# DLRM tower on one core: layer matmuls placed among those of the Gram, ids in three parts, weights loaded behind the tables

## What is computed

```python
e = jnp.stack([tbl_0[ids[:, 0]], ..., tbl_26[ids[:, 26]]], axis=1)
dot = jnp.einsum('bnd,bmd->bnm', e, e)
z = dot.reshape(2048, 27 * 27)[:, idx]      # idx: the pairs i < j
h = jnp.concatenate([z, dense_ctx], axis=1)
h = jnp.maximum(h @ W_top1 + b_top1, 0.0)
h = jnp.maximum(h @ W_top2 + b_top2, 0.0)
y = h @ W_top3
```

## Time and profile before

| | us |
|---|---|
| median of 3 runs | 417.63 (416.83 to 418.69) |
| the profiled execution | 419.41 |
| its span, first to last instruction | 417.6 |
| busy: PE / DVE / POOL / ACT | 348.4 / 276.0 / 262.4 / 159.7 |

### The profile page before, as it was taken

One profiled execution on the slowest core, in us unless ns is written; L12 is line 12 of the kernel. 1 busy time (PEld: TensorE's weight loads), 2 busy tenths in 40 slices (PEclk: granted clock), 3 DMA queues, 4 the chain that ended last, 5 costly groups with the idle time before them and its releaser, 6 DMA issues.

```text
span 417.6 us, 15062 instructions
## 1 busy us (share of the span) xinstructions
PE 348.4 (83%) x6092; PEld 312.5 (75%) x6092; DVE 276.0 (66%) x741; ACT 159.7 (38%) x221; POOL 262.4 (63%) x277
## 2 busy tenths in 40 slices
PE   0277686799979998899989998999899998899766
PEld 0266576689859897789778986898688976897565
DVE  0647954796765965896579677787479748952410
ACT  0827961223432334422442343334422334234422
POOL 5777417777477737677777767767777677770000
PEclk9978675999998999999999999999999999999889
DMA  4799995362425233245524352419333562210000
GB/s 82 176 254 249 222 82 85 65 99 64 99 54 110 52 74 84 58 90 71 113 58 102 58 111 52 109 32 85 98 75 82 66 108 56 54 53 14 3 3 0
DMA packets 29611, 35.51 MB, mean 85 GB/s; under 512 B 12729, under 2 KB 23617, under 8 KB 29586
## 3 DMA queue, kind: packets, MB, share of 16 engines
q1 hardware_dynamic: 20882, 17.32, 26.6%
q0 software_dynamic: 8704, 17.84, 15.7%
HBM read 35.13 MB, written 0.01 MB: 84 GB/s over the span
## 4 chain that ended last, share of the span: by engine, by line
PE 61%; DVE 12%; issue 10%; DMA 7%; ACT 6%; SPq 4%; ACTq 0%; DVEq 0%
PE emb_ps L579 26%; PE gram_ps L602 13%; DVE onehot L474 10%; PE mlp_ps L628 9%; PE mlp_ps L636 6%; DMA blocks<-in_tbl 4%; ACT embT L366 4%; PE emb_ps L591 3%; DMA ids_b<-in_ids_mm 3%; SPq L223 2%; PE mlp_ps L664 2%; PE mlp_ps L669 1%; DVE embT L480 1%; PE mlp_ps L612 1%; ACT h L408 1%
## 5 line engine op out<-in xcount | busy, mean ns | idle before, releaser
L333 POOL DMA_INDIRECT rows<-in_tbl,idx x272 | 262.1, 964 | 113.5 <-DMA rows<-in_tbl,idx 76.8
L474 DVE TENSOR_SCALAR onehot<-ids_b,row_of 128x256 fp32r<-128x256 int32 x616 | 188.5, 381 | 40.4 <-PE emb_ps L579 25.1
L579 PE MATMUL emb_ps<-onehot,parts 125*128 125x256 f32 x1280 | 171.4, 295 | 35.4 <-ACT parts L345 24.0
L579 PEld LDWEIGHTS emb_ps<-onehot,parts 125*128 125x128 f32 x1280 | 163.9, 200 | 40.1 <-ACT parts L345 24.7
L362 ACT ACTIVATE embT<-emb_ps 128x512 f32<-128x512 f32 x40 | 48.0, 1216 | 107.3 <-PE emb_ps L579 107.3
L602 PE MATMUL gram_ps<-embT 128*32 128x26 f32 x4096 | 56.8, 198 | 20.0 <-issue 11.6
L602 PEld LDWEIGHTS gram_ps<-embT 128*32 128x32 f32 x4096 | 47.7, 112 | 33.8 <-issue 28.3
L480 DVE COPY embT<-emb_ps 128x512 f32<-128x512 f32 (+1 forms) x32 | 31.2, 1052 | 32.2 <-PE emb_ps L591 32.2
L591 PE MATMUL emb_ps<-ident,rows 128*128 128x128 f32 x272 | 40.4, 294 | 8.1 <-ACT embT L366 7.7
L366 ACT ACTIVATE embT<-emb_ps 128x512 f32<-128x512 f32 (+1 forms) x48 | 44.6, 1076 | 1.1 <-PE emb_ps L591 1.1
L591 PEld LDWEIGHTS emb_ps<-ident,rows 128*128 128x128 f32 x272 | 32.2, 150 | 13.6 <-ACT embT L366 6.7
(11 more groups left out here) (34 smaller groups left out, 95.9 us busy)
## 6 DMA issues: line engine op xcount, KB each, us to landing
ids_b<-in_ids_mm SPq DMA_DIRECT2D x8, 768.0 KB
rows<-in_tbl,idx POOLq DMA_INDIRECT x272
ids_b<-in_ids_mm SPq DMA_DIRECT2D x8, 512.0 KB
turned<-in_tbl SPq DMA_DIRECT2D x6, 448.0 KB
h<-in_tbl SPq DMA_DIRECT2D x2, 448.0 KB
blocks<-in_tbl SPq DMA_DIRECT2D x2, 448.0 KB
w_sb<-in_W_top SPq DMA_DIRECT2D x1, 512.0 KB, 6.0
w_sb<-in_W_top SPq DMA_DIRECT2D x2, 224.0 KB
```

What stands on the lines that cost most here:

```text
L333: pool.indirect_dma_start(rows[:, t, n, :], None, tables[f], bass.IndirectOffsetOnAxis(idx[:, t, f:f + 1], 0), engine_sem=gathers_written) ...
L474: last = nc.vector.tensor_scalar(onehot[:, k % OH, c, :], ids_b[:, k, :], row_of[:, c:c + 1], None, ALU.is_equal)
L579: last = nc.tensor.matmul(emb_ps[BANK[k]][:, m * W:(m + 1) * W], parts[0:MP, f, part, c * D:(c + 1) * D], onehot[0:MP, f % OH, c, :], star ...
```

## The change

1. The ids of a pair come in three transfers (tables 0 and 1, 2 and 3, 4 to 9). In the start those of tables 2 and 3 stand behind tables 0 and 1, the last part behind tables 2 and 3, then ident; the first two parts of pair 1 come behind the tables and ahead of the weights.
2. VectorE builds the one-hots of pair 1's tables 0 to 3 at other places in pair 0: 2 and 3 behind keep_blocks of tile 0, 0 and 1 behind that of tile 1.
3. In pairs 1 to 6 only half of the first layer stands behind lookup 2. Three calls of the other half stand ahead of the wait for the copies of tile 0 and three in its Gram, behind groups 8, 16 and 24; four calls of the second layer stand ahead of the wait in tile 1 and four in its Gram, behind groups 3, 7, 11 and 15; the third layer stands behind both. ScalarE's order follows. The last pair keeps its order.

GpSimd's order stays (a helper one_queued takes over two lines), all lookups too; BUILT is 7, ids_part(k) gives the part with table k.

```diff
@@ -56,6 +56,7 @@
 NT = len(TR)
+BUILT = NM - len(ACT_ONEHOTS)
 JOBS = LOOK + TILES * NT
@@ -65,7 +66,14 @@
 ACT_JOBS = JOBS - DVE_JOBS
-IDS = [range(0, OH), range(OH, NM)]
+IDS = [range(0, 2), range(2, OH), range(OH, NM)]
+FIRST_CALLS = [3, 4]
+CALLS_AT = [(8, 16, 24), (3, 7, 11, 15)]
+def ids_part(k):
+    return sum(k >= part.stop for part in IDS)
 def row_job(t, k):
@@ -239,12 +248,12 @@
             def ids_read(p, h):
+                done = max(OH, IDS[h].stop)
                 if isinstance(p, int) and p == 0:
-                    done = IDS[h].stop
                     sp.wait_ge(onehot_act, sum(f < done for f in ACT_ONEHOTS))
                     sp.wait_ge(s_onehot, done - sum(f < done for f in ACT_ONEHOTS))
                 else:
-                    sp.wait_ge(s_onehot, p * NM - len(ACT_ONEHOTS) + IDS[h].stop)
+                    sp.wait_ge(s_onehot, BUILT + (p - 1) * NM + done)
             def load_idx(p, t):
@@ -265,11 +274,15 @@
             load_table(3)
+            load_ids(0, 2)
+            sp.dma_start(ident[:], ident_in).then_inc(s_ident, 16)
             for k in range(STAGES, NM):
                 sp.wait_ge(s_high, k - STAGES + 1)
                 sp.wait_ge(s_low, k - STAGES + 1)
                 load_table(k)
-            sp.dma_start(ident[:], ident_in).then_inc(s_const, 16)
+            for h in range(2):
+                ids_read(0, h)
+                load_ids(1, h)
             for c in range(KCH):
@@ -280,9 +293,10 @@
             def body(p, first, last):
-                if not last:
-                    ids_read(p, 0)
-                    load_ids(p + 1, 0)
+                if not last and not first:
+                    for h in range(2):
+                        ids_read(p, h)
+                        load_ids(p + 1, h)
                 if first:
@@ -301,8 +315,8 @@
                         if t == 0:
-                            ids_read(p, 1)
-                            load_ids(p + 1, 1)
+                            ids_read(p, 2)
+                            load_ids(p + 1, 2)
                 if not first:
@@ -413,10 +430,11 @@
                 elif step == 1:
-                    act.wait_ge(s_const, 16 * 5)
+                    act.wait_ge(s_const, 16 * 4)
                     bias_relu(h1, b1_sb, p, 2, (0, 1))
+                elif step == 2:
                     bias_relu(h1, b1_sb, p, 3, (2, 3))
-                elif step == 2:
+                elif step == 3:
                     bias_relu(h2, b2_sb, p, 4, (0, 1))
@@ -436,16 +454,20 @@
                         layers(p - 1, 1)
+                        if last:
+                            layers(p - 1, 2)
                 for t in range(TILES):
                     for k in range(NT):
                         if not BY_DVE[row_job(t, k)]:
                             move_rows(p, t, k)
                     if not first:
-                        layers(p - 1, 2 + t)
+                        layers(p - 1, (3 if last else 2) + t)
                     if last and t:
                         last_layers("z", 0)
                     keep_blocks(p, t, 1)
                 if not last:
+                    if not first:
+                        layers(p - 1, 4)
                     move_z(p, 0)
@@ -541,9 +563,12 @@
                         turn(p, 0)
-                    if not last:
+                    if not last and not first:
                         make_onehot(p + 1, t)
                     keep_blocks(p, t, 0)
+                    if first:
+                        make_onehot(p + 1, 2 * (1 - t))
+                        make_onehot(p + 1, 2 * (1 - t) + 1)
                 turn(p, 1)
@@ -563,7 +588,7 @@
                 if not (isinstance(p, int) and p == 0):
-                    pe.wait_ge(s_onehot, p * NM - len(ACT_ONEHOTS) + max(OH, (k + 1) * LOOK_TABLES))
+                    pe.wait_ge(s_onehot, BUILT + (p - 1) * NM + max(OH, (k + 1) * LOOK_TABLES))
                 for m in range(LOOK_TABLES):
@@ -591,9 +616,7 @@
                 done.then_inc(emb_filled, 1)
-            def gram(p, t, s):
-                step = t * STEPS + s
+            def gram(p, t, s, between=None):
                 past(pe, (gram_dve, gram_act)[s], p * TILES + t)
@@ -602,6 +625,8 @@
                                                 start=True, stop=True)
+                    if between and GS * s + g in CALLS_AT[t]:
+                        between(p - 1, FIRST_CALLS[t] + CALLS_AT[t].index(GS * s + g))
                 last.then_inc(gram_filled, 1)
@@ -612,37 +637,37 @@
                 last.then_inc(mlp_filled, 1)
-            def layers(p, step):
-                base = p * MLP_JOBS
-                if step == 0:
-                    transpose_z(p, 1)
-                elif step == 1:
...
+            def first_layer(p, half, call):
+                job, m, c = 2 + half, call // KCH, call % KCH
+                if call == 0:
+                    pe.wait_ge(mlp_moved, BANKS + p * MLP_JOBS + 2)
+                n = 2 * half + m
+                done = nc.tensor.matmul(mlp_ps[job % 2][:, m * W:(m + 1) * W],
+                                        w1_sb[0:K1[c], c, n * P:(n + 1) * P], zT[0:K1[c], c, :],
+                                        start=(c == 0), stop=(c == KCH - 1))
+                if call == 2 * KCH - 1:
+                    done.then_inc(mlp_filled, 1)
+            def first_layer_rest(p, call):
+                first_layer(p, 1, call)
+            def second_layer(p, call):
+                m, n = call // N1, call % N1
+                if call == 0:
+                    pe.wait_ge(mlp_moved, BANKS + p * MLP_JOBS + 4)
+                done = nc.tensor.matmul(mlp_ps[0][:, m * W:(m + 1) * W], w2_sb[:, n, m * P:(m + 1) * P], h1[:, n, :],
+                                        start=(n == 0), stop=(n == N1 - 1))
+                if call == N2 * N1 - 1:
+                    done.then_inc(mlp_filled, 1)
+            def third_layer(p):
+                pe.wait_ge(mlp_moved, BANKS + p * MLP_JOBS + 5)
+                for m in range(N2):
+                    done = nc.tensor.matmul(mlp_ps[1][0:1, 0:W], w3_sb[:, m:m + 1], h2[:, m, :],
+                                            start=(m == 0), stop=(m == N2 - 1))
+                done.then_inc(mlp_filled, 1)
             def last_layers(kind, t):
@@ -674,30 +699,57 @@
                 done.then_inc(mlp_filled, 1)
-            def body(p, first, last):
+            def emb_moved(p, t):
+                done = [row_job(t, k) for k in range(NT)]
+                wait_moved(pe, p, max(j for j in done if BY_DVE[j]))
+                wait_moved(pe, p, max(j for j in done if not BY_DVE[j]))
+            def lookups(p, first, last):
                 for k in range(LOOK):
                     lookup(p, k)
                     if not first and k == 0:
-                        layers(p - 1, 0)
+                        transpose_z(p - 1, 1)
                     if not first and k == 2:
-                        layers(p - 1, 1)
+                        pe.wait_ge(s_w1, 16 * sum(1 + (n % 16 > 0) for n in K1))
+                        pe.wait_ge(s_const, 16 * 4)
+                        for call in range(2 * KCH):
+                            first_layer(p - 1, 0, call)
+                        if last:
+                            for call in range(2 * KCH):
+                                first_layer(p - 1, 1, call)
+            def body(p, first, last):
+                lookups(p, first, last)
                 if first:
-                    pe.wait_ge(s_const, 16 * 5)
+                    pe.wait_ge(s_ident, 16)
                     pe.wait_ge(s_pad, 2)
                 for t in range(TILES):
                     for k in range(NT):
                         transpose_rows(p, t, k)
-                    if not first:
-                        layers(p - 1, 2 + t)
-                    done = [row_job(t, k) for k in range(NT)]
-                    wait_moved(pe, p, max(j for j in done if BY_DVE[j]))
-                    wait_moved(pe, p, max(j for j in done if not BY_DVE[j]))
-                    gram(p, t, 0)
-                    if last and t:
-                        last_layers("z", 0)
-                    gram(p, t, 1)
+                    layer = (first_layer_rest, second_layer)[t]
+                    if first:
+                        emb_moved(p, t)
+                        gram(p, t, 0)
+                        gram(p, t, 1)
+                    elif not last:
+                        for call in range(FIRST_CALLS[t]):
+                            layer(p - 1, call)
+                        emb_moved(p, t)
+                        gram(p, t, 0, layer)
+                        gram(p, t, 1, layer)
+                    else:
+                        if t == 0:
+                            for call in range(N2 * N1):
+                                second_layer(p - 1, call)
+                        else:
+                            third_layer(p - 1)
+                        emb_moved(p, t)
```

(12 more changed lines are left out.)

30 lines of the change are left out of this document (2 added, 28 removed).

## The result

The changed kernel takes 412.50 us (411.94 to 413.96, four runs) against 417.37 for the kernel before beside it: a ratio of 0.9884, with a 95% interval of 0.9849 to 0.9919. That is faster by 1.2%, in the forecast direction and inside the wide range (401.5 to 414), but outside the forecast's own (401.5 to 411): 4.9 us where the sum gave 10.6. Medians are over all executions of a kernel; the ratios leave out the slow ones (over 1.5% above the fastest of the same kernel), and those of the experiments the profiled one too, so the two can differ a little. The profiled execution took 411.94 us with a span of 410.1.

What follows compares the result with a forecast made beforehand. TensorE's order bounds the kernel, its Grams slowed by gathers pausing instructions. Terms: -9.3 (pairs 2 to 6), -3.4 (pair 1), +0.3 (start), +1.8 (pair 0) = -10.6 us, from 417.63 to 407.0; own range 401.5 to 411, 8-in-10 range 401.5 to 414.

Steps and rivals of the forecast that it cites:

- The bottleneck: Loop pairs: TensorE's order sets the 45.0 us period; its Grams run below speed because gathers pause its instruction supply.
- signs of being wrong: Gaps at gather starts between calls, TensorE waiting for rows, lookups 3 or 4 for one-hots, pair 0's lookup 4 beyond 54.
- The pauses hidden: Both Grams of a pair fall to 2.43 us, from 4.06 and 3.78: gains of 1.63 and 1.35 us.
- The price of an inner call: Entering and leaving a Gram costs 0.19 us a call, taken as upper bound; seven calls make 1.33 us a pair.
- The estimate from the Trainium skill: Weight load of each inner call: 107 ns exposed, or 0.75 us a pair instead of 1.33.
- the 0.21 of the sum: Second Gram: its 0.21 us wait for ScalarE's last copy is covered by four calls, which gives 0.21 us a pair.
- Pair 1: Pair 1 gains 3.4 us: the usual 1.86 plus 1.5, half of two long gaps totalling 3.0 us.
- Pair 0: Start: TensorE 5 us later, caught up by table 4, +0.3; wait of about 2 us before pair 1's lookup 0, +1.8.
- B: Loop and pair 1: queue fills only in part, or GpSimd becomes the bound; some 414 us; chance 0.18.
- C: Inner calls of pairs 1 to 6: each costs more than the gaps it hides; slower, 426 us; chance 0.07.
- A: Grams: pauses hide wholly and changing costs nothing; 20.0 us less, 398 us; chance 0.08.
- D: Pair 1's lookup 0: the new stop brings the 1.2 GHz level, costing 2.3 us, total 409; inside the range.

Runs made afterwards that it cites:

- e6: The changed kernel with the gathers of pairs 1 to 7 left out, rows of pair 0 used again; 415.3 us in one run.
- e3: The changed kernel with all six and all eight layer calls ahead of the Grams' waits, none inside; 415.88 us, ratio 0.992 against the kernel before.
- e11: The changed kernel with all eight second-layer calls ahead of the second Gram, three calls still in the first; 412.40 us, ratio 0.9839 against the kernel before.

## Why the prediction was right in direction and wrong in size

*The bottleneck.* Right. The Gram was the part below its speed, and the gathers were the cause, as the counterproof of the earlier trace rows said and the kernels without gathers confirmed. Of the signs of being wrong none came in the loop: no wait for rows on TensorE, none of lookups 3 and 4 for one-hots. (Lookup 4 follows 3.9 us behind lookup 3, not 4.1, so its cover was nearer 1.0 us than the 1.4 of the sum.)

*The pauses hidden.* "So I take both Grams down to the undisturbed 2.43 us" gave 2.98 us a pair over pairs 2 to 6. Of 3.43 us of pauses in pairs 3 to 6, 2.68 were hidden. The sum had looked at the 32 to 72 small matmuls between calls but not at the 128 behind the last one, and took the burst of 103 as what a filled queue carries, where it followed the beat of the gathers. That run alone keeps 0.64 us a pair. And pair 2 had pauses only in its first Gram, 1.5 us, against the full price of seven calls: there the forecast of 1.86 came out as 0.04.

*The price of an inner call.* The step that failed most. The sum took 0.19 us, from one stop in the earlier trace rows, as the upper bound. From the call's start on it did cost that (0.20; the forecast 0.62 from start to start was measured as 0.63), but another 0.10 passes ahead of it: 0.305 each, 2.14 us a pair against 1.33. The 0.81 in between is 4.9 us over six pairs, most of what the sum was off by. The sum had measured the stop of the earlier trace rows from the modelled end of the last small matmul, 395.49. That matmul starts at 395.30, so from start to start the stop is 0.75 us, not 0.56, and what passes before the transposes start was left out. (Waits for other engines stand in the code there too, so even so this row is no clean price; e6 gives it.) The estimate from the Trainium skill that stood beside it (TensorE: Matmul & The Clock Gate, Part 3, "The mechanism"; 0.107 us exposed a call) is further off, a third of the price. It is of the size of what passes ahead of a call, but no run shows that this is the load.

*A gain that the sum had almost left out.* Order alone gave 0.78 a pair (e3) against the 0.21 of the sum. With Gram and layers together at 0.54 less a pair, another 0.66 comes mostly from waits for ScalarE (0.42 less, one wait ahead of the second Gram gone and others shorter) and from the z transposes, now behind the third layer and not behind a Gram (0.25 less). This partly made up for the two terms above. In pairs 3 to 6: forecast 1.86, measured 1.20.

*Pair 1.* "1.3 us of calls in the first Gram and 1.73 in the second pass during them" failed. A long gap is time until instructions arrive, and the calls inside stand in the same stream: they can't pass. The gap at 114.46 is 2.35 us, between two calls of which neither runs in it, and the call behind it runs at the 1.2 GHz level (granted clock 0.50) and takes 1.22 us instead of 0.70. The second Gram has no long gap any more, but not for its calls: in e3, with none inside, it has none either. In the ten profiles with the layers in their new places, on chips of the usual speed, the gaps of pair 1 came to 2.0 to 4.7 us against 3.0 before, and its period was 46.95 to 52.00 against 47.82. The gain of 3.4 isn't there; -0.87 is one profile's draw.

*Pair 0.* The start went as told in kind: the first matmul at 21.34, 2.6 us later than before where the text had 5 and about 23, and caught up by lookup 4 at 51.58, 0.8 sooner than before where 52.5 was forecast. The stop before lookup 0 of pair 1 came, 1.21 us where 2 was forecast, because the builds ended at 81.37 (76.50 and 4.87), not at 82.6. What I hadn't seen is that the Gram of pair 0, although it starts sooner, ends its gap by the transfers and not by its own start. Balance +0.7, inside the bounds.

*The rivals.* B came nearest in size (414), but by half: pauses show only behind the last call, and GpSimd never became the bound; its lead lasted. C's mechanism, a call costing more than the gaps it hides, is true of the four calls in the second Gram (e11), of the loop without gathers (+0.90 a pair) and perhaps of the chips where the change costs 3%. A is out by the 0.305. D's slow lookup was seen in five profiles, but not only behind a stop, and not behind every stop.

## What to carry to other kernels

When many tiny matmuls run beside indirect gathers, look at the longest run between two long ones: here runs of 32 to 72 (0.4 to 0.75 us) lost next to nothing, one of 128 lost 0.64 us, each entry cost 0.3 us, and fewer, evenly spaced entries with no long run at the end did best in the loop. Long gaps named "issue" that stand at the same instruction in every run, in code that is written out or runs for the first time, read as waits for the instructions themselves; here they grew and ended with the data transfers ahead of them, and work in the same stream can't fill them. And price a change of kind from start to start, by the same pair of kernels with the disturbance removed: measured from a modelled end, the row of one stop left a third of it out.

## What the runs showed of the hardware that I had not expected

- The same program with gathers took 418 us on most chips and 700 to 703 on two of those used, with TensorE's supply stopping for 0.6 to 1.3 us at a time. Without gathers one of the two ran the loop at 41.07 us a pair; only the pair that still gathered was slow (79.95 us).
- Moving 768 KB of ids by 12.8 us (issued at 65.97, not 53.16) moved a stop of TensorE with it: 4.16 and 2.16 us in the two Grams of pair 0 became 0.83 and 7.23. The stops stood at the same small matmuls, the 167th of one Gram and the 147th of the next, whatever their length.
- The small matmuls run 9.1 ns apart when nothing disturbs them (256 from 259.36 to 261.69 without gathers), and 0.12 us pass from the start of the last one to that of a long one. A gather pauses them twice, at its start and 0.46 us later, for some 0.2 us each.
